# The last 512 tokens of a routed feed-forward run through all eight experts ahead of the item loop

## The chip, the cores and the metric

The kernel runs on one core of one Trainium2 chip. The metric is the device time of one execution in microseconds (us). Engines: PE is TensorE, DVE VectorE, ACT ScalarE, POOL GpSimd, SP the engine that issues most DMAs.

## What is computed

```python
h = _layernorm(x, axis=-1) * (1 + ca) + sa             # x: (2, 2048, 128)
x = x + ga * attention_block(h, Wq, Wm, W1, W2, g1, b1, g2, b2)   # linear attention and an MLP
h = _layernorm(x, axis=-1) * (1 + cb) + sb
x = x + gb * ffn(h, Wg, W1, W2)

def ffn(x, Wg, W1, W2):                                # Wg (128, 8), W1 (8, 128, 256), W2 (8, 256, 128)
    probs = softmax(xt @ Wg)                           # 4096 tokens, 8 experts
    _, top_idx = top_k(probs.T, 512)                   # each expert picks its 512 best tokens
    masked = where(sel, probs.T, -inf)
    tok2exp = where(sel.any(0), argmax(masked, 0), argmax(probs.T, 0))
    weights = probs[token, tok2exp]
    for e in range(8):
        gate = where(tok2exp == e, weights, 0)
        out += gate[:, None] * (gelu(xt @ W1[e], exact) @ W2[e])
```

So every token goes through exactly one expert, weighted by its probability. How many tokens an expert gets is known only on the chip. ga, gb and the other modulations come from a small matmul.

## The kernel before

All numbers are fp32. The 4096 tokens lie as 32 tiles of 128 (NT = 32), in 8 groups of 4 tiles (G, GT). The kernel has five engine programs, written out by hand in the order in which each engine executes; semaphores tie them.

**Attention and router (up to 137 us).** Each engine walks over the groups, software-pipelined. Results: x_sb (the stream after attention), h2 (the input of the experts), the router's logits in a bank of PSUM, and at the end h2T, the last two groups of h2 transposed. SP writes x_sb and h2 of each group to a table in DRAM (`table`, 256 numbers a token), POOL computes h2 for it (L348, L349) while the search runs.

**Search (from 140 us).** For each expert the 512th largest probability is found bit by bit, three bits a round, in ten rounds: DVE counts keys under four candidates (L1044), ACT under three (L517, Sign with a sum), PE adds the counts over partitions (L730, L733), DVE picks the digit (L1054, L1058). After round 0 ACT also casts the low halves of the keys (L522).

**Selection.** DVE finds which tokens each expert keeps, each token's expert, its rank within the expert by a scan along the tile, and with PE's sums over partitions (L735 to L754; `rbase_ready`) its slot in a list sorted by expert. Then the list is inverted with one-hot matrices: DVE builds them in four quarters of 8 tiles (L1120 to L1123), PE multiplies (L759), and DVE reads which token stands in each slot (L1136 to L1138: `gidx`). Before that read, DVE computes `eid`, the expert of each item (L1127 to L1133). A second pass of the same kind (`ohit`, `ohw`, L1149 to L1151, PE L794) gives the weight of every slot and item (L1156 to L1158).

**Item loop.** The sorted list is cut into 32 tiles. A tile that holds the end of an expert's tokens is run once for each expert in it, so there are at most NI = 32 + 7 = 39 items, and always 39 are run. Item i uses expert e = eid[i] and tile i - e. Per tile POOL gathers 128 rows of the table (L369, 16 of them ahead: R = 16), PE transposes them (p_xt, L766), ACT copies the result out of PSUM (L530). Per item SP loads the expert's W1 (L221, up to RW = 4 ahead), PE does the up matmuls (p_up, L773), ACT the GELU (L534), PE the down matmuls with W2 held in SBUF (p_down, L782), and DVE adds the weighted result to the tile's sum (add_item, L1166). From item LAG = 7 on, DVE also finishes tile i - 7 (finish, L1171 to L1178), and POOL scatters it to the output (L373) and then issues the gather of 16 tiles later:

```python
            for t in range(NT):
                gp.wait_ge(S["o_done"], t + 1)
                scatter(t)
                if t + R < NT:
                    gather(t + R)
```

PE's order in the loop is p_up(i + 1), p_xt(i + 2), p_down(i), and a down matmul waits until DVE has added item i - 2 (`y_free`):

```python
            for i in range(NI):
                e_next = p_up(i + 1) if i + 1 < NI else None
                if i + 2 < NT:
                    p_xt(i + 2)
                p_down(i, e_now)
                e_now = e_next
```

## Time and profile before

| | us |
|---|---|
| median of 3 runs (310.49 to 312.85) | 312.84 |
| the profiled execution | 311.66 |
| its span | 309.9 |
| PE busy in the span | 177.5 (57%) |
| DVE busy | 200.9 (65%) |
| ACT busy | 98.5 (32%) |
| POOL busy | 161.0 (52%) |

The span runs from the first to the last instruction of the profile; the execution's own time is 1.8 us longer. Times in rows are counted from the span's start. "Idle before" is the time in which the engine did nothing before this instruction, with the instruction that released it; "issue" means that the profile shows nothing that it waited for, "remote" an unknown source. In the table by stage, each engine's busy time stands with the number of its instructions, and PEclk is the granted share of PE's 2.4 GHz. An fp32 matmul stands as two records, so "x4" in rows of PE is two matmuls.

### The profile page before, as it was taken

What the parts mean: (1) busy time and instruction counts of PE and PEld (TensorE: products, weight loads), DVE (VectorE), ACT (ScalarE), POOL (GpSimd) and SP (SyncE); (2) the same over time, 40 slices, a digit from 0 to 9 for tenths busy, and PEclk for the clock granted to TensorE, in tenths of its full rate; (3) what the DMA queues carried; (4) which work ended last, traced back from release to release, by engine and by line L of the source; (5) the groups of instructions that cost most, each with busy time, mean ns of one, the idle gap of its engine ahead of it and who ended that gap; (6) DMA issues with size and microseconds to landing.
All of it is one profiled execution on the core that took longest, in us unless ns stands there. A gap on an engine that the chain in (4) does not pass through costs nothing.

```text
span 309.9 us, 4483 instructions
## 1 busy us (share of the span) xinstructions
PE 177.5 (57%) x1035; PEld 145.2 (47%) x1035; DVE 200.9 (65%) x701; ACT 98.5 (32%) x338; POOL 161.0 (52%) x229
## 2 busy tenths in 40 slices
PE   0878896596798895351112033527754574588730
PEld 0546684575586585351001022426644464577520
DVE  3789839949999988658897997013533253346660
ACT  1189843144265463115564002002221121222200
POOL 8645278917555334406991006770076665735552
PEclk9999997778699799555555555755995765758995
DMA  6940000000100000002662003432243333324210
GB/s 156 257 132 2 1 0 0 2 0 1 36 0 1 2 1 0 2 0 68 188 186 69 0 0 120 121 118 69 79 118 96 101 107 97 119 78 121 93 36 17
DMA packets 21721, 20.08 MB, mean 65 GB/s; under 512 B 2624, under 2 KB 19008, under 8 KB 21696
## 3 DMA queue, kind: packets, MB, share of 16 engines
q1 hardware_dynamic: 18144, 13.24, 14.7%
q0 software_dynamic: 2560, 6.30, 6.7%
q10 hardware_dynamic: 992, 0.27, 0.9%
q8 instruction: 9, 0.15, 0.2%
q14 instruction: 16, 0.13, 0.1%
HBM read 13.51 MB, written 6.29 MB: 64 GB/s over the span
## 4 chain that ended last, share of the span: by engine, by line
DVE 33%; PE 29%; another core or an unknown queue 13%; POOL 8%; issue 7%; ACT 6%; DMA 1%; DVEq 1%; POOLq 1%; ACTq 0%
PE pH L773 9%; DVE x_sb L965 6%; DVE hT L1044 5%; PE pQ L782 4%; POOL yr L244 3%; PE pH L675 3%; DVE bn L817 2%; ACT u L534 2%; PE pQ L668 2%; PE pQ L685 2%; POOL rs L244 2%; DVE xn L825 2%; PE pQ L567 2%; ACT x_sb L530 1%
## 5 line engine op out<-in xcount | busy, mean ns | idle before, releaser
L773 PE MATMUL pH<-x_sb,hid 128*128 (+1 forms) x156 | 35.9, 366 | 36.1 <-ACT x_sb L530 26.3
L373 POOL DMA_INDIRECT out_dram<-u,gidx x32 | 32.1, 1005 | 41.8 <-DVE u L1178 31.5
L369 POOL DMA_INDIRECT xn<-table_dram,gidx x32 | 33.6, 1051 | 33.2 <-DVE gidx L1138 23.8
L1166 DVE SCALAR_TENSOR_TENSOR h<-pQ,wslot,h 128x128 f32 (+1 forms) x39 | 13.7, 351 | 57.4 <-PE pQ L782 21.5
L773 PEld LDWEIGHTS pH<-x_sb,hid 128*128 128x128 f32 x156 | 27.1, 246 | 43.4 <-issue 43.4
L534 ACT ACTIVATE u<-pH 128x256 f32<-128x256 f32 x39 | 15.0, 384 | 80.7 <-remote 36.4
L782 PE MATMUL pQ<-ew,u 128*128 (+1 forms) x156 | 31.4, 337 | 3.9 <-issue 2.6
L782 PEld LDWEIGHTS pQ<-ew,u 128*128 128x128 f32 x156 | 27.6, 249 | 5.0 <-issue 4.7
L965 DVE SCALAR_TENSOR_TENSOR x_sb<-u,yr,x_sb 128x128 f32<-128x128 f32 x64 | 24.6, 445 | 4.4 <-POOL yr L244 4.1
L479 ACT ACTIVATE sqj<-pQ 128x128 bf16<-128x128 f32 x64 | 16.9, 278 | 28.4 <-POOL yr L244 12.3
L243 POOL TENSOR_SCALAR ve<-mv 128x4 f32<-128x4 f32 x16 | 3.3, 205 | 36.5 <-DVE mv L820 36.3
L825 DVE TENSOR_SCALAR xn<-x_sb,mv,rs 128x128 f32<-128x128 f32 x64 | 17.4, 336 | 3.5 <-POOL rs L244 3.5
L675 PE MATMUL pH<-qT,mall 128*128 128x512 f32 x32 | 19.0, 724 | 0.0
L685 PEld LDWEIGHTS pQ<-w,hid 128*128 128x128 f32 x128 | 16.0, 197 | 6.0 <-issue 6.0
L817 DVE BATCH_NORM_STATS2 bn<-x_sb 128x6 f32<-128x128 f32 x64 | 13.9, 280 | 6.1 <-DMA x_sb<-in_L_attn_x_dram 5.8
L685 PE MATMUL pQ<-w,hid 128*128 128x128 f32 x128 | 16.0, 280 | 1.9 <-DVE u L955 1.9
L668 PE MATMUL pQ<-mall,qT 128*128 128x128 f32 x64 | 12.2, 352 | 8.6 <-DVE u L950 8.6
L244 POOL TENSOR_TENSOR rs<-ve,neghalf 128x4 f32<-128x4 f32 x16 | 16.2, 1015 | 1.3
L348 POOL TENSOR_TENSOR t<-xn,cbR 128x512 f32<-128x512 f32 x8 | 10.1, 1266 | 11.2 <-DVE khi L1034 10.2
L668 PEld LDWEIGHTS pQ<-mall,qT 128*128 128x128 f32 x64 | 10.9, 255 | 9.9 <-issue 6.1
L244 POOL TENSOR_TENSOR yr<-yv,neghalf 128x8 f32<-128x8 f32 x8 | 13.1, 1639 | 0.7
L479 ACT ACTIVATION_READ_ACCUMULATOR sqj<-pQ 128x1 f32 x64 | 13.2, 207 | 0.0
(275 smaller groups left out, 441.2 us busy)
## 6 DMA issues: line engine op xcount, KB each, us to landing
hid<-in_L_ffn_W_dram SPq DMA_DIRECT2D x39, 128.0 KB
x_sb<-in_L_attn_x_dram SPq DMA_DIRECT2D x8, 256.0 KB, 6.5
table_dram<-x_sb SPq DMA_DIRECT2D x8, 256.0 KB, 2.8
table_dram<-h SPq DMA_DIRECT2D x8, 256.0 KB, 2.3
ew<-in_L_ffn_W_dram SPq DMA_DIRECT2D x2, 512.0 KB, 7.6
xn<-table_dram,gidx POOLq DMA_INDIRECT x32
out_dram<-u,gidx POOLq DMA_INDIRECT x32
wmod_sb<-in_L_wmod_dram SPq DMA_DIRECT2D x1, 384.0 KB, 4.9
```

What stands on the lines that cost most here:

```text
L244: return gp.tensor_tensor(dst, tmp, neghalf[:, 0:width], ALU.pow)
L369: gp.indirect_dma_start(row[:, t % R, :], None, table[:, :], bass.IndirectOffsetOnAxis(gidx[:, t:t + 1], 0), bounds_check=B * L - 1, oob_i ...
L373: gp.indirect_dma_start(out.rearrange("b l d -> (b l) d"), bass.IndirectOffsetOnAxis(gidx[:, t:t + 1], 0), o_sb[:, t % RO, :], None, bound ...
L479: last = act.activation(sqj[:, g % 2, k * GT + t, :], pQ[k][:, t * D:(t + 1) * D], ACT.Square, accum_out=ssq[:, g % 2, k * GT + t:k * GT + ...
L534: act.activation(eh[:, i % 2, :], pH[i % 2][:, 0:F], ACT.Gelu).then_inc(S["eh_done"], 1)
L668: mm = te.matmul(pQ0[:, t * D:(t + 1) * D], qT[:, g % 2, t * P:(t + 1) * P], mall[:, b, 0:D], start=True, stop=True)
L675: mm = te.matmul(pH[f][:, :], mall[:, b, D + f * P:D + (f + 1) * P], qT[:, g % 2, :], start=True, stop=True)
L685: mm = te.matmul(pQ1[:, t * D:(t + 1) * D], hid[:, g % 2, f, t * P:(t + 1) * P], w2[:, f, :], start=(f == 0), stop=(f == 1))
L773: mm = te.matmul(pH[i % 2][:, f * P:(f + 1) * P], wcur[:, i % RW, f * P:(f + 1) * P], xt[:, bass.ds(i - e, 1), :], start=True, stop=True)
L782: mm = te.matmul(pQ[i % 2][:, 0:D], eh[:, i % 2, f * P:(f + 1) * P], ew[:, bass.ds(e, 1), f * D:(f + 1) * D], start=(f == 0), stop=(f == 1))
L825: last = dve.tensor_scalar(xn[:, g, t, :], x_sb[:, g * GT + t, :], mv[:, g, t, 0:1], rs[:, g, t:t + 1], ALU.subtract, ALU.mult)
L965: last = dve.scalar_tensor_tensor(x1, u[:, t, :], yr[:, g % 2, n + t:n + t + 1], x1, ALU.mult, ALU.add)
```

## The change

The last group (tokens of tiles 28 to 31, DG = 7) leaves the sorted list and goes through all eight experts.

- **PE**: 16 up matmuls of 128x512 (`d_up`, weights w1d, input h2T of the last group) and 8 down steps of eight 128x128 matmuls (`d_down`). One such step stands after each round of the search, and the others between the matmuls of the selection and after the slot matmuls.
- **ACT**: 16 GELUs (`d_gelu`) and 8 copies out of PSUM (`d_copy`) in the same places. The activation table of GELU is loaded ahead of the search, no longer at the first item.
- **DVE**: during items 1 to 11 the eight results are summed with their weights (`dense_step`), multiplied by gb and added to x_sb.
- **SP**: loads all of W1 once (1 MB, at the start); stores the finished group in the loop, after the weight load of item 14.
- The list has 28 tiles (NP) and NI = 35 items, so 28 gathers and scatters. The quarters have 8, 8, 6 and 6 tiles.
- DVE reads the slots before it computes `eid`, and the weight pass is done in two halves, the first ahead of the first item's matmuls.
- POOL leaves out h2 of the last group; SP writes x_sb in its place.

```diff
-NI = NT + E - 1
+NI = NT - GT + E - 1
-NB = NT // 2
-QUARTERS = 4
+NP = NT - GT
+NB = NP // 2
+QUARTERS = (4, 4, 3, 3)
+DG = G - 1
...
+        def up_bank(k):
+            return (pH0, pQ1, pF)[k % 3]
...
+                if i == NP // 2:
+                    sp.wait_ge(S["out_d"], 1)
+                    sp.dma_start(out.rearrange("b (p t) d -> b p t d", p=P)[B - 1, :, TB - GT:TB, :], bgroup(x_sb, DG))\
+                      .then_inc(S["stored_d"], 16)
...
+            def d_gelu(k):
+                e = k // 2
+                act.wait_ge(S["up_d"], k + 1)
+                if e >= 2:
+                    act.wait_ge(S["down_d"], e - 1)
+                act.activation(ehd[e % 2][:, k % 2, :], up_bank(k)[:, :], ACT.Gelu).then_inc(S["gelu_d"], 1)
+
+            def d_copy(e):
+                act.wait_ge(S["down_d"], e + 1)
+                act.copy(yde[e], pQ0[:, :].rearrange("p (t d) -> p t d", d=D)).then_inc(S["copy_d"], 1)
+
+            d_gelu(0)
+            between = ((d_gelu, 1), (d_gelu, 2), (d_gelu, 3), (d_copy, 0), (d_gelu, 4), (d_gelu, 5), (d_copy, 1), (d_gelu, 6),
+                       (d_gelu, 7), (d_copy, 2))
...
+            def d_up(k):
+                e, f = k // 2, k % 2
+                if k >= 3:
+                    te.wait_ge(S["gelu_d"], k - 2)
+                te.matmul(up_bank(k)[:, :], w1d[:, e, f * P:(f + 1) * P], h2T[:, DG % 2, :], start=True, stop=True,
+                          skip_group_check=True).then_inc(S["up_d"], 1)
+
+            def d_down(e):
+                te.wait_ge(S["gelu_d"], 2 * e + 2)
+                if e:
+                    te.wait_ge(S["copy_d"], e)
+                for t in range(GT):
+                    for f in range(2):
+                        mm = te.matmul(pQ0[:, t * D:(t + 1) * D], ehd[e % 2][:, f, t * P:(t + 1) * P], ew[:, e, f * D:(f + 1) * D],
+                                       start=(f == 0), stop=(f == 1), skip_group_check=True)
+                mm.then_inc(S["down_d"], 1)
...
+            between = ((d_up, 2), (d_up, 3), (d_down, 0), (d_up, 4), (d_up, 5), (d_down, 1), (d_up, 6), (d_up, 7), (d_down, 2),
+                       (d_up, 8))
...
+            te.wait_ge(S["copy_d"], E)
...
+            p_weights(0)
             e_now = p_up(0)
...
+            link(dve.tensor_copy(inv[:, 0:2, 0:NP], pG[:, 0:2 * NP].rearrange("p (v j) -> p v j", v=2)))
+            link(dve.tensor_tensor(idf[:, 0:NP], inv[:, 0, 0:NP], inv[:, 1, 0:NP], ALU.add))
+            dve.tensor_copy(gidx[:, 0:NP], idf[:, 0:NP]).then_inc(S["slots_done"], 1)
+
             dve.wait_ge(S["rbase_ready"], 2)
...
+                    e = k - 1
+                    for t in range(GT):
+                        if e == 0:
+                            last = dve.tensor_scalar(accd[:, t, :], yde[e][:, t, :], wd[:, t, e:e + 1], None, ALU.mult)
+                        else:
+                            last = dve.scalar_tensor_tensor(accd[:, t, :], yde[e][:, t, :], wd[:, t, e:e + 1], accd[:, t, :], ALU.mult, ALU.add)
+                    last.then_inc(S["acc_d"], 1)
...
-                if i < 6:
+                if i < 5:
                     dve.memset(yacc[:, 8 + 4 * i:12 + 4 * i, :], 0.0)
+                if 1 <= i <= E + 3:
+                    dense_step(i - 1)
```

PE, rounds 1 to 3 of the search, before. L730 opens the sum in bank pG, L733 adds the counts.

```order
L730 MATMUL pG<-fill,onesb 128x7 [waits digits]
L733 MATMUL pG<-cnt,same16b 128x7 [waits counts,acounts]
L730 MATMUL pG<-fill,onesb 128x7 [waits digits]
L733 MATMUL pG<-cnt,same16b 128x7 [waits counts,acounts]
L730 MATMUL pG<-fill,onesb 128x7 [waits digits]
L733 MATMUL pG<-cnt,same16b 128x7 [waits counts,acounts]
```

The same three rounds now. L778 is an up matmul, L787 a down step.

```order
L804 MATMUL pG<-fill,onesb 128x7 [waits digits]
L807 MATMUL pG<-cnt,same16b 128x7 [waits counts,acounts]
L778 MATMUL pH<-h2T,w1d 128x512 [waits gelu_d]
L804 MATMUL pG<-fill,onesb 128x7 [waits digits]
L807 MATMUL pG<-cnt,same16b 128x7 [waits counts,acounts]
L787 MATMUL pQ<-ew,ex 128x128 [waits gelu_d]
L787 MATMUL pQ<-ew,ex 128x128 x7
L804 MATMUL pG<-fill,onesb 128x7 [waits digits]
L807 MATMUL pG<-cnt,same16b 128x7 [waits counts,acounts]
L778 MATMUL pQ<-h2T,w1d 128x512 [waits gelu_d]
```

Each round has gained an operation between the sum of its counts and the opening of the next. PE in the selection, from the last sums for the threshold (L742, L744) to the first slot matmuls (L759), before:

```order
L742 MATMUL pL<-scan,before 128x16 [waits rsum_ready]
L744 MATMUL pL<-scan,onesb 128x8
L748 MATMUL pF<-shift,onesb 128x16
L750 MATMUL pF<-rank,bmo 128x16 [waits rank_ready]
L752 MATMUL pF<-csum,onesb 128x16
L754 MATMUL pQ<-csum,onesb 128x8
L759 MATMUL pG<-feat,featT 128x64 [waits hi_ready] x32
```

And now (L830 is the matmul on the ranks, L843 the slot matmuls):

```order
L821 MATMUL pL<-scan,onesb 128x8
L787 MATMUL pQ<-ew,qT 128x128 [waits copy_d,gelu_d]
L787 MATMUL pQ<-ew,qT 128x128 x7
L778 MATMUL pQ<-h2T,w1d 128x512 [waits gelu_d]
L778 MATMUL pF<-h2T,w1d 128x512 [waits gelu_d]
L787 MATMUL pQ<-ew,ex 128x128 [waits copy_d,gelu_d]
L787 MATMUL pQ<-ew,ex 128x128 x7
L828 MATMUL pT<-shift,onesb 128x16
L830 MATMUL pT<-rank,bmo 128x16 [waits rank_ready]
L832 MATMUL pT<-csum,onesb 128x16
L834 MATMUL pH<-csum,onesb 128x8
L778 MATMUL pH<-h2T,w1d 128x512 [waits gelu_d]
```

Two down steps and two ups stand ahead of the matmul on the ranks, and one up (with a down step behind it) ahead of the slot matmuls. DVE, one early item of the loop (L1163 reads the item's expert), before:

```order
L1163 TENSOR_LOAD eid [waits y_free]
L1163 ISA x2
L1166 ISA [waits y_ready]
L1166 SCALAR_TENSOR_TENSOR h<-pQ,wslot,h 128x128
L1187 MEMSET h 128x512
```

And now:

```order
L1264 TENSOR_LOAD eid [waits y_free]
L1264 ISA x2
L1267 ISA [waits y_ready]
L1267 SCALAR_TENSOR_TENSOR h<-pQ,wslot,h 128x128
L1312 MEMSET h 128x512
L1288 SCALAR_TENSOR_TENSOR u<-feat,wd,u 128x128 [waits acc_d]
L1288 SCALAR_TENSOR_TENSOR u<-feat,wd,u 128x128 x3
```

Four operations on 128x128 follow the add and its memset.

## Rows read from the trace of the kernel before

**Rows 1.** Table by stage: us from and to, length, busy time of each engine, PEclk, DMA

```profile
137.00:187.00 50.00, 7.92 (x65) 5.16 (x65) 43.77 (x188) 17.30 (x64) 20.23 (x16) 0.50 0.27 79
187.00:211.00 24.00, 8.71 (x56) 7.62 (x56) 6.46 (x17) 3.18 (x8) 17.05 (x16) 0.57 0.41 121
228.00:275.00 47.00, 26.08 (x125) 23.39 (x124) 16.71 (x56) 7.90 (x28) 29.89 (x30) 0.66 0.35 105
```

**Rows 2.** Timeline of the search (start, us, engine, line, operation, idle before)

```profile
141.72 0.51 ACT L517 ACTIVATE hT<-khi,cur 128x256 bf16<-128x256 f32 x1 [3.10 <-DVE khi L1034]
...
148.60 0.17 PE L733 MATMUL pG<-cnt,same16b 128*128 128x7 bf16 x1 [1.63 <-DVE hT L1044]
149.29 0.19 PE L730 MATMUL pG<-fill,onesb 128*128 128x7 bf16 x1 [0.53 <-DVE cur L1058]
149.33 0.51 ACT L517 ACTIVATE hT<-khi,cur 128x256 bf16<-128x256 f32 x1 [0.92 <-DVE cur L1058]
...
151.11 0.17 PE L733 MATMUL pG<-cnt,same16b 128*128 128x7 bf16 x1 [1.62 <-DVE hT L1044]
```

**Rows 3.** Timeline of POOL in the loop, and one of the sums of ACT's waits

```profile
208.01 1.00 POOL L369 DMA_INDIRECT xn<-table_dram,gidx  x1 [0.30 <-issue]
224.36 1.02 POOL L373 DMA_INDIRECT out_dram<-u,gidx  x1 [15.35 <-DVE u L1178]
...
271.38 1.03 POOL L369 DMA_INDIRECT xn<-table_dram,gidx  x1 [0.30 <-issue]
...
ACT u L534 <- remote: 36.4, 7, 8.8
```

**Rows 4.** DVE: timeline of the loop; a group of the lines; a piece of the chain

```profile
213.99 0.35 DVE L1166 SCALAR_TENSOR_TENSOR h<-pQ,wslot,h 128x128 f32 x1 [1.95 <-PE pQ L782]
...
222.23 0.35 DVE L1166 SCALAR_TENSOR_TENSOR h<-pQ,wslot,h 128x128 f32 x1 [1.29 <-PE pQ L782]
...
273.77 0.35 DVE L1166 SCALAR_TENSOR_TENSOR h<-pQ,wslot,h 128x128 f32 x1 [5.66 <-PE pQ L782]
...
301.37 0.35 DVE L1166 SCALAR_TENSOR_TENSOR h<-pQ,wslot,h 128x128 f32<-128x128 f32 x1 [0.34 <-issue]
...
L1187 DVE MEMSET h<- 128x512 f32 x6 | 2.9, 485 | 0.3
...
126.56 1.15 DVE x_sb L965 x4
```

**Rows 5.** Chain (59 to 65 us), timeline of PE (88 to 91 us), one group of ACT

```profile
59.54 2.05 PE pQ L668 x8
61.59 3.41 PE pH L675 x4
...
88.17 1.88 PE L675 MATMUL pH<-qT,mall 128*128 128x512 f32 x4
89.89 1.95 PE L685 MATMUL pQ<-w,hid 128*128 128x128 f32 x16
...
L472 ACT ACTIVATE hid<-pH 128x512 f32<-128x512 f32 x8 | 4.8, 605 | 5.7 <-PE pH L675 5.6
```

**Rows 6.** Timeline from the last quarter to the first item

```profile
183.98 0.61 PE L759 MATMUL pG<-feat,featT 128*128 128x64 bf16 x8 [0.73 <-DVE featT L1123]
...
185.81 0.22 DVE L1136 COPY inv<-pG 128x64 f32<-128x64 f32 x1
...
187.39 1.30 POOL L369 DMA_INDIRECT xn<-table_dram,gidx  x1 [23.77 <-DVE gidx L1138]
...
190.70 0.45 PE L766 MATMUL pT<-ident,xn 128*128 128x128 f32 x1 [6.12 <-DMA xn<-table_dram,gidx]
...
191.53 1.28 ACT L534 ACT_TABLE_LOAD   x1
```

**Rows 7.** Timeline of PE around the ranks and the first two quarters

```profile
176.11 0.20 PE L750 MATMUL pF<-rank,bmo 128*128 128x16 bf16 x1 [5.22 <-DVE csum L1096]
...
179.98 0.61 PE L759 MATMUL pG<-feat,featT 128*128 128x64 bf16 x8 [3.63 <-DVE featT L1123]
181.31 0.61 PE L759 MATMUL pG<-feat,featT 128*128 128x64 bf16 x8 [0.73 <-DVE featT L1123]
```

More of the change, by code:

```diff
@@ L261, in _ @@
             gp.memset(segmask[:, :], 1.0)
+            gp.memset(oh[:, :, B - 1, TB - GT:TB], 0.0)
             gp.memset(same16b[:, :], 1.0)
@@ L360, in _ @@
             gp.wait_ge(S["keys"], 1)
-            for g in range(G):
+            for g in range(DG):
                 h2tok(g)
@@ L522, in _ @@
                     act.copy(klo[:, :], ki[:, 1, :]).then_inc(S["klo_ready"], 1)
+                step, what = between[n]
+                step(what)
             act.wait_ge(S["over_ready"], 1)
@@ L1150, in _ @@
-            for v in range(3):
-                last = dve.tensor_tensor(ohw[:, :, v, :, :], ohit[:, :, :, :], pair(val[:, 2 + v, :], NI), ALU.mult)
-            last.then_inc(S["ohw_ready"], 1)
+            half = NB // 2
+            for h in range(2):
+                bs, ts = slice(h * half, (h + 1) * half), slice(2 * h * half, 2 * (h + 1) * half)
+                link(dve.tensor_tensor(ohit[:, bs, :, :], count_to(NI, half), pair(item[:, ts], NI), ALU.is_equal))
+                for v in range(3):
+                    last = dve.tensor_tensor(ohw[:, bs, v, :, :], ohit[:, bs, :, :], pair(val[:, 2 + v, ts], NI), ALU.mult)
+                last.then_inc(S["ohw_ready"], 1)
```

173 lines of the change are left out of this document (118 added, 55 removed).

## The prediction, made before the changed kernel was run

> **What bounds the kernel now.** I read the table by stage first. From 137 to 187 us (search and selection) TensorE (PE) is busy 7.92 of 50.00 us, at a granted clock of 0.50, which is 1.2 of 2.4 GHz, and DVE 43.77 us: DVE's chain sets this stage [rows 1]. Next, the timeline of one search round: the matmul that sums the counts (L733) starts at 148.60 and again at 151.11, so a round is 2.51 us; PE idles 1.62 us right before it, and ACT 0.92 us before the first of its three count operations [rows 2]. Those gaps are where the new work goes. From 187 us on, the item loop. PE is busy only 8.71 of 24.00 us up to 211 and 26.08 of 47.00 us from 228 to 275 [rows 1]; ACT waits 36.4 us in 7 pieces for something that the profile doesn't name [rows 3]. These stretches coincide with the gathers: item 2 is added only at 213.99, right after the first 16 gathers, and from the first scatter at 224.36 to the last gather at 271.38 the loop again goes slowly [rows 3, 4]. DVE's adds at 222.23 (item 7) and 273.77 (item 23) lie 51.54 us apart, 3.22 us an item. After that, with no gather left, items 23 to 38 take 27.60 us, 1.84 us each, which is DVE's own pace [rows 4]. So a slot that needs no gather inside the loop is worth 3.22 us, but one after the gathers only 1.84.
>
> **The change, part by part.** The change adds one end of the work (512 tokens through eight experts) and takes four items off the other.
>
> *Prices of one dense step.* An up matmul is 128x512 fp32. Two cost 3.41 us at the low clock and 1.88 at the high one, so 1.71 or 0.9 us each. A down step is eight 128x128 matmuls: 1.95 us for eight at the high clock; at the low one four took 2.05 us, so 4.1. One GELU or copy over 512 columns on ACT is like L472: 0.6 us [rows 5].
>
> *Search.* In rounds with an up matmul PE needs 1.71 us at most, and between one L733 and the next there are 2.51 less 0.17 and 0.19, so 2.15 us: hidden at either clock. A down step stands in three rounds. At 1.95 us it is hidden; at 4.1 us each makes its round 1.9 us late. That is 0 to 5.7 us; I take 2.0, as the clock should be high for part of it. On ACT a 0.6 us operation fits into the gap of 0.92 us, except in round 0, where ACT also casts the low keys: 0.6 us late. First GELU and table load: ACT idles 3.10 us before the first count operation, and the load of 1.28 us plus 0.6 fit; it was beside the first item before, where it delayed little: 0 [rows 2, 6]. Search: +2.6 us.
>
> *Selection.* Before its matmul on the ranks (L750, 176.11) PE idles 5.22 us [rows 7]. Two downs and two ups now stand there: 5.7 us at the high clock, 11.6 at the low one. So L750, for which DVE waits with everything behind it, is 0.5 to 6.4 us late; I take 1.5, plus 0.2 for the up matmuls beside the threshold. Behind L750 one up and one down come before the first slot matmul, which is 3.87 us later (179.98) [rows 7]: 2.9 us fit, 5.8 do not. Two more ups stand between the quarters, whose pitch is 1.33 us. I take 0.5 late at the end. Two gains: the quarters shrink from 32 tiles and 64 columns to 28 and 56, about 0.8 of 5.3 us; and DVE reads the slots (L1136, 185.81) as soon as PE has them. Now the last quarter's matmul ends at 184.59 (183.98 + 0.61) and DVE first computes the piece numbers; 1.2 us go [rows 6]. Gathers start at +2.6 + 1.7 + 0.5 - 0.8 - 1.2 = **+2.8 us**.
>
> *Start of the loop.* After the slot matmuls PE still owes one up, two downs and the waits for ACT's two copies, 0.9 + 3.9 + 1.2 = 6.0 us, and only then comes the first transpose (now at 190.70). The slot matmuls would end at 184.59 + 2.8 + 1.2 = 188.6, so the transpose at 194.6: 3.9 us late, against a first gather that lands 3.3 us after its start [rows 6], at 193.5. But items 0 to 2 are held until the 16 gathers are through, and these are 2.8 late. So +2.8 stands for item 2 as well. The halved weight pass has its matmuls in the same slow stretch: 0.
>
> *Dense sums on DVE.* Eight steps of four operations, 1.15 us a step as in L965 [rows 4], about 1.25 with its wait, in items 2 to 9, and smaller ones in items 1, 10 and 11. From item 2 to item 7 the loop has 8.24 us, 1.65 an item, PE's pace, in which DVE has an idle gap ahead of each add: 1.29 us in item 7, where no memset stands, of which some 0.6 are the reading of the piece number. Where a memset of 0.485 us also stands, little is free [rows 4]. Three items at about +1.0 and two at +0.55: **+4.1 us**. For items 7 to 11 DVE has added 1.25 us each while PE is being held anyway, and DVE has up to two finished items in hand: I take +1.0 of 0 to 5.
>
> *SP.* After the weight load of item 14 SP waits for the dense sum (item 11 on DVE), then stores 256 KB, and the loads of items 15 and later are queued behind. PE is at most two items ahead of DVE, so a load that now comes four items early comes just in time: 0 to 3 us, I take 0.5. POOL loses one pair of operations in the search: 0, it is not waited for.
>
> *Four items less.* They go out of the stretch at 3.22: the gathers within the loop fall from 16 to 12, and the 16 items behind the last gather remain. 4 x 3.22 = **-12.9 us**; at the tail's pace it would be 4 x 1.84 = -7.4.
>
> *Sum.* 2.8 + 4.1 + 1.0 + 0.5 - 12.9 = -4.5 us, against the profiled execution of 311.66 us (span 309.9): 307.2, call it **307 us**. The median of the runs shown is 312.84, so that is 1.9% below it.
>
> **The clock, and one rule of the skill that speaks against the change.** The row of 137 to 187 us shows 0.50 with PE almost idle; from 228 to 275, with PE busy just over half, it is 0.66 [rows 1]. The Trainium skill, TensorE: Matmul & The Clock Gate, Part 1, says the default state is throttled and activity releases it. By it the dense work would lift its own clock, but must first run slow; if it never lifts, the sum is that of the first rival. The Trainium skill, ScalarE: Activation LUTs, What ACT_TABLE_LOAD costs, gives about 2.66 us a switch with its drain, the trace 1.28 for the load; by the page the first count operation would be some 0.2 us late. ACT's order has one such load before and after, so GELU between the counts brings no more.
>
> **The rivals.**
> *The clock stays low (slower).* PE's dense work then overruns every gap: 0.6 + 5.7 in the search, 6.4 + 0.9 around the ranks, 2.0 at the quarters, less 2.0 gained: +13.6 us for the gathers, in place of 2.8. Total 311.66 + 13.6 + 5.6 - 12.9 = 318.0. For it: 50 us at 0.50. Against: with 16 ups and 8 downs PE has 60 us of low-clock work, so it would hardly idle. It decides once the start is later than +12.
>
> *The saved items are worth the tail's pace (no change).* If the slow stretch is set by something else than the count of gathers, four items give 7.4: 311.66 + 8.4 - 7.4 = 312.7. For it: the engines are held by a cause that I can't name. Against: nothing slows the loop once the gathers are over.
>
> *All is hidden (faster still).* At the high clock the gathers start 0.6 - 2.0 = -1.4 us, stage costs 4.1 + 1.0: 311.66 - 1.4 + 5.1 - 12.9 = 302.5. Against: one down at the low clock is enough to lose 1.9 us.
>
> **How the numbers follow.** Forecast 0.45, clock low 0.15, tail's pace 0.20, all hidden 0.20. Beyond about 1% (3.1 us) a difference can be told from none. The forecast spreads by the search (0 to 5.7), the ranks (0.5 to 6.4), SP (0 to 3) and DVE (0 to 5), and is faster by over 1% in some 85 of 100. Faster 0.38 + 0.20 + 0.02 = 0.60; same 0.06 + 0.16 = 0.22; slower 0.15 + 0.03 = 0.18. The range reaches from below the third rival, 300, to 316, which leaves out most of the first.
>
> **What would show it.** Rounds of 2.5 us in the search except those with a down step (up to 4.4); a granted clock above 0.50 from about 145 us; the idle time of DVE before its read of the rank sums; gathers starting near 190; items 3 to 9 at 2.2 to 3.1 us on DVE; 12 gathers within the loop and 16 items of 1.84 us behind them. I am wrong if the gathers start before 188 or after 195, if DVE's dense steps cost the loop under 2 or over 8 us, or if the stretch with gathers takes as long with 12 of them as with 16.

## The result, and the profile after

The changed kernel takes **299.50 us** (median of 4 runs, 299.04 to 300.37), the kernel before in the same session 312.85 us (310.49 to 314.11). The ratio is 0.9591, 95% interval 0.9549 to 0.9633: 4.1% less. The prediction was 307.0 us, range 300 to 316. So the sign was right, the gain between the profiled executions (12.1 us) was nearly three times the forecast 4.5, and the time lies just under the range.

| | before | after |
|---|---|---|
| profiled execution, us | 311.66 | 299.52 |
| span, us | 309.9 | 297.8 |
| mean granted clock of TensorE | 0.749 | 0.828 |
| first gather issued, us | 187.39 | 186.19 |
| item 2 added | 213.99 | 214.21 |
| item 7 added | 222.23 | 222.45 |
| last gather issued | 271.38 | 260.47 |
| last item added | 301.37 | 289.87 |

The table by stage of the kernel after (us from and to, length, busy time and instructions of PE, PEld, DVE, ACT and POOL, granted clock, DMA share, GB/s), against [rows 1]:

```profile
137.00:187.00 50.00, 38.43 (x205) 24.46 (x204) 42.45 (x191) 30.34 (x87) 18.53 (x15) 0.83 0.28 80
187.00:211.00 24.00, 8.80 (x68) 7.52 (x67) 5.76 (x19) 2.74 (x8) 15.77 (x16) 0.67 0.41 121
228.00:265.00 37.00, 20.08 (x96) 17.02 (x96) 16.08 (x53) 5.83 (x21) 24.05 (x23) 0.70 0.36 111
```

In search and selection TensorE is busy 38.43 us in place of 7.92, at a mean granted clock of 0.83 in place of 0.50, and DVE's own 42.45 us still fill the stage.

The timelines of PE and ACT in the search, kernel after (start, us, engine, line, operation, idle before), against [rows 2, 5, 6]:

```profile
138.62 1.28 ACT L538 ACT_TABLE_LOAD   x1
...
141.70 0.51 ACT L554 ACTIVATE hT<-khi,cur 128x256 bf16<-128x256 f32 x1 [1.19 <-DVE khi L1127]
```

```profile
148.86 0.17 PE L807 MATMUL pG<-cnt,same16b 128*128 128x7 bf16 x1 [0.42 <-DVE hT L1137]
148.88 3.03 PE L787 MATMUL pQ<-ew,ex 128*128 128x128 f32 x16
...
157.64 3.60 PE L787 MATMUL pQ<-ew,qT 128*128 128x128 f32 x16
...
166.27 2.02 PE L787 MATMUL pQ<-ew,ex 128*128 128x128 f32 x16
...
176.89 0.19 PE L830 MATMUL pT<-rank,bmo 128*128 128x16 bf16 x1
```

L787 is a down step. Two of the three in the search ran partly at the low clock (3.03 and 3.60 us) and the third at the high one (2.02 us). The granted clock over these stretches (table by stage, columns as above):

```profile
146.00:149.00 3.00, 2.25 (x6) 0.86 (x6) 2.30 (x13) 2.67 (x10) 2.78 (x3) 0.50 0.69 200
149.00:152.00 3.00, 3.00 (x20) 2.99 (x20) 2.24 (x13) 1.78 (x8) 2.78 (x3) 0.67 0.71 199
155.00:158.00 3.00, 0.92 (x6) 0.56 (x5) 2.72 (x14) 2.06 (x7) 2.78 (x3) 0.97 0.70 200
158.00:160.00 2.00, 2.00 (x12) 2.00 (x11) 1.96 (x10) 1.59 (x6) 1.78 (x3) 0.50 0.54 153
162.00:187.00 25.00, 20.16 (x143) 13.97 (x141) 22.43 (x94) 12.95 (x34) 0.81 (x1) 1.00 0.11 31
```

It came up during the first down step, fell back by the second, after PE had been busy for only 0.92 us from 155 to 158, and was full from 162 on. The table load and the first GELU ended before ACT's first count operation, which starts at 141.70 as before at 141.72. The rank matmul is 0.78 us later than before (176.89 against 176.11, [rows 7]).

From the last quarter to the first gather, kernel after (timelines of DVE and POOL), against [rows 6]:

```profile
184.62 0.21 DVE L1229 COPY inv<-pG 128x56 f32<-128x56 f32 x1
```

```profile
186.19 1.50 POOL L392 DMA_INDIRECT xn<-table_dram,gidx  x1 [25.32 <-DVE gidx L1231]
...
206.34 1.00 POOL L392 DMA_INDIRECT xn<-table_dram,gidx  x1 [0.30 <-issue]
225.63 1.01 POOL L396 DMA_INDIRECT out_dram<-u,gidx  x1 [18.29 <-DVE u L1303]
226.95 1.04 POOL L392 DMA_INDIRECT xn<-table_dram,gidx  x1 [0.30 <-issue]
...
251.16 1.01 POOL L396 DMA_INDIRECT out_dram<-u,gidx  x1 [3.67 <-DVE u L1303]
...
260.47 1.03 POOL L392 DMA_INDIRECT xn<-table_dram,gidx  x1 [0.30 <-issue]
```

The gathers start 1.2 us earlier than before, not 2.8 later. In the loop, the stretch from the first scatter to the last gather is 260.47 - 225.63 = 34.84 us for 12 gathers; before it was 271.38 - 224.36 = 47.02 us for 16 [rows 3]. That is 2.90 and 2.94 us a pair of scatter and gather. From the last gather to the last add it is 29.40 us, before 29.99. The whole difference of 11.5 us at the last add is then: first scatter 1.27 later, this stretch 12.18 shorter, the rest 0.59 shorter. Of the 12.18 us some 10.3 are eight steps fewer of POOL, and 1.9 are pauses of POOL (5.7 us of them before, 3.8 after). From the issue of the last scatter to the end of the span it is 5.86 us, before 6.51, which is another 0.65 us.

DVE's adds, kernel after, against [rows 4] (items 2, 7, 12 and 34):

```profile
214.21 0.35 DVE L1267 SCALAR_TENSOR_TENSOR h<-pQ,wslot,h 128x128 f32 x1 [0.94 <-PE pQ L872]
...
222.45 0.35 DVE L1267 SCALAR_TENSOR_TENSOR h<-pQ,wslot,h 128x128 f32 x1
...
236.22 0.35 DVE L1267 SCALAR_TENSOR_TENSOR h<-pQ,wslot,h 128x128 f32 x1 [0.70 <-issue]
...
289.87 0.35 DVE L1267 SCALAR_TENSOR_TENSOR h<-pQ,wslot,h 128x128 f32<-128x128 f32 x1 [0.34 <-issue]
```

Item 2 to item 7 takes 8.24 us, exactly as before, though five items now carry steps of the dense sum.

### The profile page after: what moved, and what is told of

Its sections match the earlier page's. It is cut to its first block, busy times and chain, and to the rows that moved or that the text cites. A ratio compares the mean times of both kernels' runs of the same rounds, so it can differ in the third digit from the quotient of the medians.

```text
span 297.8 us, 4671 instructions
## 1 busy us (share of the span) xinstructions
PE 200.4 (67%) x1151; PEld 156.1 (52%) x1151; DVE 202.8 (68%) x725; ACT 108.9 (37%) x354; POOL 150.0 (50%) x220
## 4 chain that ended last, share of the span: by engine, by line
PE 34%; DVE 30%; issue 17%; POOL 8%; ACT 5%; another core or an unknown queue 2%; DVEq 1%; POOLq 1%
PE pH L863 7%; DVE x_sb L1058 6%; PE pQ L787 5%; DVE hT L1137 4%; POOL yr L266 3%; PE pQ L872 3%; PE pH L726 3%; DVE bn L910 3%; PE pQ L719 2%; PE pQ L736 2%; POOL rs L266 2%; DVE xn L918 2%; ACT u L585 2%; PE pQ L618 2%
## 5 line engine op out<-in xcount | busy, mean ns | idle before, releaser
L863 PE MATMUL pH<-x_sb,hid 128*128 (+1 forms) x140 | 30.8, 354 | 31.5 <-issue 21.5
L396 POOL DMA_INDIRECT out_dram<-u,gidx x28 | 28.5, 1017 | 41.0 <-DVE u L1303 30.4
L392 POOL DMA_INDIRECT xn<-table_dram,gidx x28 | 29.0, 1035 | 33.5 <-DVE gidx L1231 25.3
L863 PEld LDWEIGHTS pH<-x_sb,hid 128*128 128x128 f32 x140 | 23.1, 235 | 38.3 <-issue 38.3
L585 ACT ACTIVATE u<-pH 128x256 f32<-128x256 f32 x35 | 13.4, 383 | 74.7 <-PE pH L863 31.0
L1267 DVE SCALAR_TENSOR_TENSOR h<-pQ,wslot,h 128x128 f32 (+1 forms) x35 | 12.3, 350 | 38.2 <-PE pQ L872 13.7
L872 PE MATMUL pQ<-ew,u 128*128 (+1 forms) x140 | 26.9, 324 | 7.0 <-issue 4.4
L872 PEld LDWEIGHTS pQ<-ew,u 128*128 128x128 f32 x140 | 23.1, 234 | 9.1 <-issue 8.8
L502 ACT ACTIVATE sqj<-pQ 128x128 bf16<-128x128 f32 x64 | 16.8, 277 | 28.4 <-POOL yr L266 12.2
L265 POOL TENSOR_SCALAR ve<-mv 128x4 f32<-128x4 f32 x16 | 3.3, 204 | 36.5 <-DVE mv L913 36.4
L719 PE MATMUL pQ<-mall,qT 128*128 128x128 f32 x64 | 12.1, 351 | 8.6 <-DVE u L1043 8.6
L371 POOL TENSOR_TENSOR t<-xn,cbR 128x512 f32<-128x512 f32 x7 | 8.9, 1267 | 11.0 <-DVE khi L1127 10.2
## 6 DMA issues: line engine op xcount, KB each, us to landing
w1d<-in_L_ffn_W_dram SPq DMA_DIRECT2D x1, 1024.0 KB, 10.3
```

Source lines behind the costliest of these rows:

```text
L392: gp.indirect_dma_start(row[:, t % R, :], None, table[:, :], bass.IndirectOffsetOnAxis(gidx[:, t:t + 1], 0), bounds_check=B * L - 1, oob_i ...
L396: gp.indirect_dma_start(out.rearrange("b l d -> (b l) d"), bass.IndirectOffsetOnAxis(gidx[:, t:t + 1], 0), o_sb[:, t % RO, :], None, bound ...
L502: last = act.activation(sqj[:, g % 2, k * GT + t, :], pQ[k][:, t * D:(t + 1) * D], ACT.Square, accum_out=ssq[:, g % 2, k * GT + t:k * GT + ...
L719: mm = te.matmul(pQ0[:, t * D:(t + 1) * D], qT[:, g % 2, t * P:(t + 1) * P], mall[:, b, 0:D], start=True, stop=True)
L863: mm = te.matmul(pH[i % 2][:, f * P:(f + 1) * P], wcur[:, i % RW, f * P:(f + 1) * P], xt[:, bass.ds(i - e, 1), :], start=True, stop=True)
L872: mm = te.matmul(pQ[i % 2][:, 0:D], eh[:, i % 2, f * P:(f + 1) * P], ew[:, bass.ds(e, 1), f * D:(f + 1) * D], start=(f == 0), stop=(f == 1))
```

## The experiments

They ran on two chips (one for runs 1 to 4, one for runs 5 to 12), and the first thing they showed is that the ground had changed: the kernel before takes 283.9 us on the one and 284.6 us on the other, in place of 312.85. Which chip the first measurement ran on is not on record; the texts call it the first chip. The ratio of the change is the same. The kernels before and after were therefore profiled again, as runs 5 and 6. In the expectations, a "chip like the first" is one at 312.85 us.

The ratio behind each time is to the kernel before of the same session, with its 95% interval. The changed kernel itself was not run again on the chip of runs 1 to 4, so for these runs "under the changed kernel" sets their time against run 6 on the other chip, and a difference under about 1.5 us is not clear of noise (the intervals reach 0.4 to 0.6% to either side). One profiled execution also differs from the next ahead of the loop: the same code issued its first gather between 185.74 and 187.18 us in nine of them (kernel after, and runs 1 to 3, 6 to 8, 11 and 12).

**Runs 5 and 6: the kernels before and after again.** No edit.

> The kernel before, unchanged, for its profile on the chip of these experiments. On the chip of the first experiments it took 283.9 us instead of 312.85. If what went is the late signals of TensorE during the gathers, the first item is added 6.5 us after the first gather was issued plus the gather's own latency, near 196 us (213.99 in the first profile, item 2), items 0 to 7 go at 1.7 us each, and POOL issues a scatter and a gather each 2.65 us without a pause between the first scatter and the last gather, which ends items 16 on. On a chip like the first one it is 311 to 313 us with item 2 at 214.

> The changed kernel, unchanged. Ratio to before 0.95 to 0.96 whichever chip it is: about 271.5 us where before takes 284, 299.5 where it takes 312.85. Theory P (in the loop POOL's chain of indirect transfers, 1.31 us each, is what the four tiles cost: 8 transfers, 10.5 us) and theory I (the items cost what the items cost, 1.82 us each, 7.3 us for four) both have to reach the difference of 12 us: under P POOL's pause between issues is nil up to the last gather and items 16 on wait for gathers.

Measured: before 284.61 us (ratio 0.9994, 0.9969 to 1.0019), after **272.15 us** (0.9562, 0.9522 to 0.9602). The same first 190 us as on the first chip, and then a loop without its stalls. ACT's timeline, first the kernel after on the first chip, then the same kernel here (L585 is the GELU of an item, which waits for the up matmuls):

```profile
196.58 0.38 ACT L585 ACTIVATE u<-pH 128x256 f32<-128x256 f32 x1 [5.23 <-remote]
...
208.62 0.38 ACT L585 ACTIVATE u<-pH 128x256 f32<-128x256 f32 x1 [11.50 <-remote]
```

```profile
192.53 0.38 ACT L585 ACTIVATE u<-pH 128x256 f32<-128x256 f32 x1 [1.22 <-PE pH L863]
...
194.18 0.38 ACT L585 ACTIVATE u<-pH 128x256 f32<-128x256 f32 x1 [1.11 <-PE pH L863]
```

So the waits of 36.4 us for something unnamed [rows 3] are not a property of the kernel. POOL's transfers in the loop, kernel before, then kernel after, on this chip (timelines):

```profile
208.13 1.00 POOL L369 DMA_INDIRECT xn<-table_dram,gidx  x1 [0.30 <-issue]
212.14 1.02 POOL L373 DMA_INDIRECT out_dram<-u,gidx  x1 [3.01 <-DVE u L1178]
213.46 1.04 POOL L369 DMA_INDIRECT xn<-table_dram,gidx  x1 [0.30 <-DVE u L1178]
...
253.43 1.03 POOL L369 DMA_INDIRECT xn<-table_dram,gidx  x1 [0.30 <-issue]
...
276.63 0.98 POOL L373 DMA_INDIRECT out_dram<-u,gidx  x1 [0.59 <-issue]
```

```profile
209.91 1.01 POOL L396 DMA_INDIRECT out_dram<-u,gidx  x1 [2.18 <-DVE u L1303]
...
241.49 1.03 POOL L392 DMA_INDIRECT xn<-table_dram,gidx  x1 [0.30 <-issue]
...
264.71 0.98 POOL L396 DMA_INDIRECT out_dram<-u,gidx  x1 [0.59 <-issue]
```

Each transfer holds POOL about 1.0 us, and the next starts 0.30 us behind it: a scatter and a gather take 2.65 us. Before, POOL runs so without a pause from 212.14 to past 253.43 (the 15 pairs between its first and last gather in the loop take 39.97 us, 2.66 each), while the items could go at 1.82 us. From there to the end both kernels need the same: the last add stands 21.15 us behind the issue of the last gather before, and 21.16 after. The first add came at 198.34 us in run 5, 2.3 us later than expected. DVE's adds show the price of the dense sums, which have no stalls to hide behind here: item 7 to item 12 takes 9.16 us before (210.01 to 219.17) and 13.74 us after (206.73 to 220.47).

**Run 1: no late weight loads.** 

```
             for i in range(NI):
-                e = sp.value_load(...)
-                if i >= RW:
-                    sp.wait_ge(S["up_ready"], i - RW + 1)
-                sp.dma_start(wcur[:, i % RW:i % RW + 1, :], ...)
                 if i == NP // 2:
                     ...                                    # the store of the finished group, as before
+                if i >= RW:
+                    continue
+                e = sp.value_load(...)
+                sp.dma_start(wcur[:, i % RW:i % RW + 1, :], ...)
```

> The changed kernel, with the loop's weight loads on SP left out after the first four items, so later items use the first weights still in the buffers (left out: the right W1 of items 4 to 34; all transfers of 128 KB on SP's queue after the fourth go). Theory G (the gathers of POOL alone set the pace of items 7 to 19): within 1% of 299.5 us, items 7 to 20 still take some 42 us. Theory W (gathers and weight loads share the transfer engines, and it is their sum that holds): 10 to 20 us less, items 7 to 20 at 2.0 to 2.5 us each.

Measured: 272.43 us (0.957, 0.9516 to 0.9624) against 272.15 for the changed kernel: no difference. The weight loads don't set the time, but one of them is late in the loop. SP waits for the dense sum before it stores the finished group, and the next weight load stands behind that store (issued at 218.89 and 219.99 us in run 6). PE waits for it:

```profile
223.00 1.22 PE L863 MATMUL pH<-x_sb,hid 128*128 x4 [3.27 <-DMA hid<-in_L_ffn_W_dram]
```

Items 12 to 14 take 5.07 us in run 6 and 3.64 here, where that load is left out. The 1.4 us are lost again by the end, as the gathers are as late (runs 2 and 3). The expected 42 us for items 7 to 20 were those of the first chip (41.88); here they are 28.4 us.

**Run 2: no gathers in the loop.** 

```
             for t in range(NP):
                 gp.wait_ge(S["o_done"], t + 1)
                 scatter(t)
-                if t + R < NP:
-                    gather(t + R)
```

> The changed kernel without the 12 gathers that POOL issues inside the loop; the tiles 16 to 27 take the rows of tiles 0 to 11 (left out: the fetch of those rows). If the gathers in the loop hold items 7 to 19 (my prediction's 3.22 us for each item against 1.82 without them), these 13 items go at 1.82 to 1.9 us and the time is 284 us, 15 less. If the loop is held by the chain PE, ACT, DVE of an item, less than 3 us comes off. Items 0 to 2, behind the first 16 gathers, stay where they are in either case.

PE's wait for a gather is adapted to it. Measured: 270.72 us (0.9514, 0.9465 to 0.9562), only 1.4 us under the changed kernel. From item 16 on the items go at 1.82 us, yet nearly the same end is reached. So after the change the gathers in the loop are hardly a bound any more: something else is as late. Run 3 shows what.

**Run 3: no dense sums on DVE.** 

```
-                if 1 <= i <= E + 3:
-                    dense_step(i - 1)
```

SP's wait for the dense sum ahead of the store goes with them.

> The changed kernel without the eleven steps on DVE that weigh and sum the experts' outputs of the last 512 tokens (left out: those sums; the store of these tokens stays, and no longer waits). The dense work on PE and ACT stays. My prediction's term for these steps was 4.1 us in items 2 to 7: by it item 7 ends 4 us earlier and the time is 295 to 296 us. By the reading of the trace after (item 2 to item 7 took 8.24 us with and without them) item 7 moves by under 0.5 us and the time stays within 0.5% of 299.5 us.

Measured: 271.05 us (0.9533, 0.9475 to 0.9592), 1.1 us less, not clear of noise. Inside it moves more than that. Item 7 is where it was (207.65 us, 206.73 in run 6, whose loop began 0.9 us earlier), so the steps at items 1 to 6 are free, as the trace after had said. But item 7 to item 12 takes 9.16 us in place of 13.74: the five steps at items 7 to 11, where the output operations stand as well, cost 0.92 us each. Items 12 to 14 take 3.64 us in place of 5.07, as the late weight load of run 1 is gone too. Most of these 6.0 us is given back later: item 20 to item 24 alone takes 10.69 us in place of 7.42, each add waiting for a row whose gather POOL has only just issued. The timeline of PE in run 3:

```profile
236.56 0.71 PE L862 MATMUL pH<-x_sb,hid 128*128 x4 [0.45 <-issue]
238.40 0.48 PE L855 MATMUL pF<-ident,xn 128*128 128x128 f32 x1 [1.14 <-DMA xn<-table_dram,gidx]
```

**Run 4: no dense work.** All calls of `d_up`, `d_gelu`, `d_down`, `d_copy` and `dense_step` left out.

> The changed kernel with no dense work at all (left out: the experts of the last 512 tokens, on PE, ACT and DVE; the loop has 35 items as before the edit). My prediction charged that work 2.6 us in the search, 1.9 us of lateness in ranks and quarters, 2.8 us at item 2 and 4.1 us for the sums: by it the first gather starts some 4 us earlier and the time is about 291 us. By the reading of the trace after, where the clock was already up for most of it, the search ends 0.9 us earlier, the first gather starts 0.5 to 1.0 us earlier (185.3 us), unless the engine's clock falls without that work, and the time is 298 to 299 us.

Measured: 269.42 us (0.9462, 0.9412 to 0.9511), 2.7 us under the changed kernel, more than the 0.5 to 1.5 us expected. The first gather starts at 185.49 against 186.13. The search and selection stage:

```profile
137.00:187.00 50.00, 7.50 (x61) 4.81 (x61) 43.71 (x194) 17.28 (x64) 19.19 (x15) 0.50 0.27 79
```

PE's 31 us of dense work cost the gathers 0.64 us between these two executions, and by the spread of the nine others 0.3 to 1.7. Of the 9.9 us that my prediction's terms put on the dense work (2.6 + 1.7 + 0.5 + 4.1 + 1.0), 2.7 reach the end, through POOL: its last gather is issued at 238.89 in place of 241.49.

**Run 7: eight more gathers.** The kernel after, with POOL's count of indirect transfers back at 64, and nothing else.

```
                 if t + R < NP:
                     gather(t + R)
+                if t < 8:
+                    gp.indirect_dma_start(spare[t], None, table[:, :],
+                                          bass.IndirectOffsetOnAxis(gidx[:, t:t + 1], 0), ...)
```

> The changed kernel with eight more indirect gathers on POOL, one behind each of the first eight scatters, into buffers that nobody reads: POOL issues again 64 indirect transfers, as before the change; items, tiles and all other work stay at 35. Theory P (POOL's chain sets the end): 8 x 1.31 = 10.5 us slower, 282 us or 310 us, as slow as before within 1%. Theory I (the four items themselves): the same as the changed kernel within 1%.

Measured: **283.31 us**, 11.2 us slower than the changed kernel, and within 0.5% of the kernel before (0.9954, 0.9932 to 0.9977). Theory P holds: give POOL its eight transfers back and the gain is gone, although four items, their weights, their matmuls and their outputs stay away. What is left of the gain, 1.3 us, is about the earlier start of the gathers. POOL in this run:

```profile
209.84 1.02 POOL L398 DMA_INDIRECT out_dram<-u,gidx  x1 [2.18 <-DVE u L1308]
211.16 1.05 POOL L394 DMA_INDIRECT xn<-table_dram,gidx  x1 [0.30 <-issue]
212.52 1.01 POOL L410 DMA_INDIRECT pe_<-table_dram,gidx  x1 [0.31 <-issue]
...
275.11 0.98 POOL L398 DMA_INDIRECT out_dram<-u,gidx  x1 [0.59 <-issue]
```

From first gather to last scatter it is 275.11 - 186.16 = 88.95 us, before (run 5) 276.63 - 187.56 = 89.07, after (run 6) 264.71 - 186.13 = 78.58. The difference of the last two is 10.49 us, which is 8 x 1.31. The rest of the 11.2 us stands behind the last scatter: from its issue to the end of the span it is 6.52 us here and in run 5, and 5.86 in run 6. That piece goes by the number of indirect transfers in every trace (4.88 us with 44 of them, 5.21 with 48, 5.86 with 56, 6.51 or 6.52 with 64), 0.08 us for each.

**Run 8: the dense sums early.** 

```
+DENSE = {0: (2,), 1: (3,), 2: (4,), 3: (5,), 4: (6,), 5: (7, 8), 6: (9, 10)}
...
-                if 1 <= i <= E + 3:
-                    dense_step(i - 1)
+                for k in DENSE.get(i, ()):
+                    dense_step(k)
```

Steps 0 and 1 stand ahead of the wait for the weights (`inv_ready`, 3).

> The changed kernel with the DVE steps of the dense sums moved ahead: steps 0 and 1 in DVE's wait ahead of the loop, the others at items 0 to 6, so that none stands beside the output steps of items 7 to 11. The result is the reference's. Items 7 to 12 then go at 1.83 us in place of 2.75 (4.6 us earlier at item 12). Theory P: gathers of POOL hold items 16 to 26 instead, and 1 to 2 us of it remain in the time. Theory D (DVE holds the loop): 4 us remain. On a chip like the first, item 7 is late by the signals of TensorE, and 0 to 4 us remain.

Measured: 271.90 us (0.9552, 0.9513 to 0.9591), the same as the changed kernel within its uncertainty. Item 7 is 1.7 us later (208.44), item 12 is 2.3 us earlier (218.17), and items 20 to 24 take 10.54 us where POOL has not yet issued their gathers. Less than the 1 to 2 us of theory P is left; theory D is out.

**Run 9: one part of the change alone.** The kernel before, with the slots (`inv`, `idf`, `gidx`) read ahead of `endi`, `enext`, `eid`, the first operations on the weights moved ahead of that read, and the weight pass in two halves.

> The kernel before with one part of the change alone: slots read ahead of the piece numbers and the weight pass in two halves (all four tiles of the last 512 tokens stay sparse; the result is the reference's). The first gather should start 1.2 us earlier (186.3 in place of 187.56). Theory P (POOL's chain of 64 indirect transfers runs from there almost without a pause to the last scatter): the time falls by the same 1.0 to 1.3 us, 283.4 where before takes 284.6. If the start is not on the path (items wait elsewhere in between): no change, within 0.2%.

Measured: 282.63 us (0.9926, 0.9903 to 0.9949), 2.1 us less, more than the 1.2 expected. The first gathers of run 5 and of run 9:

```profile
187.56 1.30 POOL L369 DMA_INDIRECT xn<-table_dram,gidx  x1 [23.74 <-DVE gidx L1138]
```

```profile
185.72 1.56 POOL L369 DMA_INDIRECT xn<-table_dram,gidx  x1 [22.57 <-DVE gidx L1136]
```

1.84 us earlier, of which 1.17 are the order (POOL's wait is 23.74 and 22.57 us); in the rest (0.65 us) the two executions differ already before the edit, at the first slot matmul. Of the 1.84 us, 1.57 are left at the last scatter (275.06 against 276.63): the start is on the path. The medians' 2.1 us (1.4 to 2.8 by the interval) is more than the 1.17 of the order, and why is open. The halved weight pass seems to help too: item 0 is added 2.82 us earlier (195.52 against 198.34), more than the gathers' 1.84, and POOL's pause ahead of its first scatter falls from 3.01 to 2.44 us.

**Run 10: the kernel before without gathers in the loop.** The edit of run 2, on the kernel before.

> The kernel before without the 16 gathers inside the loop; later tiles take rows of earlier ones (left out: the fetch of these rows). Theory P: items 16 to 38 go at 1.82 us in place of 2.16 on the mean (226.96 to 274.58), the last item is added near 267, 8 us earlier, and the time is 276 to 277 us; items alone bound it then, and the four that the change saves would be worth 7.3 us. If the items' own chain holds it: under 2 us.

Measured: 275.45 us (0.9666, 0.9633 to 0.9699), 9.2 us under before; the last item is added at 266.84 in place of 274.58. Beside run 2 this makes a square: with the gathers in the loop the change gives 284.61 - 272.15 = 12.5 us, without them 275.45 - 270.72 = 4.7 us (runs 10 and 2, on two chips whose kernel before differs by 0.8 us). The latter is what the items alone give, by the adds of runs 10 and 2: item 7 is added 2.84 us earlier, the items behind item 14 take 7.50 us less, being four fewer, the sums at items 7 to 11 take 4.65 more and the late weight load 0.95: together 4.74.

The square also bounds theory P. With 39 items and not one gather in the loop the kernel takes 275.45 us, 3.3 us more than the changed kernel with its 56 transfers. So by run 10 a change that only took eight transfers away could give 9.2 us at most; the rest of the 12.5 comes from items that start earlier and are four fewer.

**Run 11: gathers ahead of scatters.**

```
-            for t in range(NP):
-                gp.wait_ge(S["o_done"], t + 1)
-                scatter(t)
-                if t + R < NP:
-                    gather(t + R)
+            for t in range(NP - R):
+                gp.wait_ge(S["o_done"], t + 1)
+                gather(t + R)
+                if t % 2:
+                    scatter(t // 2)
+            for t in range((NP - R) // 2, NP):
+                gp.wait_ge(S["o_done"], t + 1)
+                scatter(t)
```

> The changed kernel, with POOL issuing each loop gather ahead of the scatters (two gathers, then one scatter, until the last gather; then the other scatters); the result is the reference's. The last gather should be issued near 233 in place of 241.5 us. POOL's chain stays 56 x 1.31 us long, so it ends 0 to 3 us earlier, as its pauses are closed. Since without any loop gather the time fell by 1.4 us only, items and DVE hold it as well: 270.5 to 271.5 us where the changed kernel takes 272.15.

Measured: 274.55 us (0.964, 0.9605 to 0.9674), **2.4 us slower** than the changed kernel; my expectation was wrong. The scatters held back left POOL with nothing to do while items came at 2.88 us (the dense sums) and while PE waited for the late weight load of run 1 (4.30 us here, 3.27 in run 6), and they are owed at the end:

```profile
210.10 0.99 POOL L392 DMA_INDIRECT xn<-table_dram,gidx  x1 [1.94 <-DVE u L1306]
212.98 1.00 POOL L392 DMA_INDIRECT xn<-table_dram,gidx  x1 [1.88 <-DVE u L1306]
...
265.67 0.98 POOL L396 DMA_INDIRECT out_dram<-u,gidx  x1 [0.30 <-issue]
266.96 0.98 POOL L396 DMA_INDIRECT out_dram<-u,gidx  x1 [0.30 <-issue]
```

The last scatter follows the one before it by 1.29 us: POOL is still catching up when the last item is done (263.90). It comes 3.06 us behind the last add, in run 6 2.06. So of 2.25 us at the last scatter 1.0 are owed scatters, and 1.25 stand already at the last add; they arise at items 12 to 16, behind the late weight load. That the order of the transfers lengthened this wait fits but is not shown. From 228.74 us on POOL issues without a longer pause than 0.50 us, so a pause before that is not made good, as theory P says.

**Run 12: both edits.** Run 8 and run 11 together.

> Both edits together: gathers ahead of scatters and the dense sums on DVE at items 0 to 6; the result is the reference's. Theory P with a second bound beside it (each edit alone gains little because the other bound is as late): together items 12 to 34 go at 1.82 us, the last item is added at 218.2 + 22 x 1.82 = 258.2, POOL's chain then ends some 3 us earlier than now, near 262, and the time is 268.5 to 269.5 us, 2.5 to 3.5 less. If only the sum of single gains holds: 270.5 to 271.

Measured: **269.69 us** (0.9487, 0.9454 to 0.952), 2.5 us under the changed kernel, though run 8 alone gained nothing and run 11 alone lost. The last item is added at 257.66, 5.0 us earlier, and the last scatter is issued at 261.69, 3.0 us earlier. That is 0.2 us above the expected range, and every run of it is below every run of the single edits (269.28 to 270.75 against 271.64 and more). From first gather to last scatter it is 75.95 us; 55 steps of 1.31 are 72.1, and of the 4 us between them only 1.2 are pauses, the rest are transfers that held POOL longer. The last scatter comes 4.0 us behind the last add, in run 6 2.06, so POOL's chain ends this version, and fewer transfers could bring some 2 us before the items, at 1.82 us each from item 12 on, hold it. It is the best version found.

## Why the prediction was wrong

Two steps of the sum failed: the dense sums on DVE in items 2 to 7, priced at +4.1 us, cost nothing, and the delay of item 2, priced at +2.8 us, was 0.22. The parts in order:

- **Search, +2.6 us.** The later end of the search is 0.93 us (the threshold is ready at 169.33 against 168.40). The mechanism was right: the rounds with a down step that ran partly at the low clock (3.03 and 3.60 us) are 0.4 and 1.1 us longer, where I had charged 1.9 for each step at the low clock. The third step ran at the high clock and cost nothing. Of ACT's 0.6 us 0.23 came, in round 0. The table load made nothing late: GELU starts 1.29 us behind the load's start (139.91), and the first count operation is on time, so the 0.2 us named for a drain did not come. That makes 1.7 us, and 0.7 of them were given back by luck. One DVE operation halfway (L1064, now L1157) takes 1.30 us before and 0.61 after, and in both ends at 155.65, some 0.3 us behind the end of the POOL operation beside it (155.37 and 155.36):

```profile
154.35 1.30 DVE L1064 SCALAR_TENSOR_TENSOR klo<-khi,cur,klo 128x256 f32<-128x256 f32 x1
...
155.04 0.61 DVE L1157 SCALAR_TENSOR_TENSOR klo<-khi,cur,klo 128x256 f32<-128x256 f32 x1
```

  With this work the granted clock of the stage is 0.83. By the Trainium skill, TensorE: Matmul & The Clock Gate, Part 1, activity releases the throttle; the trace agrees (0.50 without this work, run 4, and 0.83 with it).
- **Ranks and quarters, +1.7 and +0.5.** Mis-sized: next to nothing. The four steps ahead of the ranks ran at the high clock, as in the lower end of my range. The rank matmul is 0.78 us later, which is less than the search was.
- **Slots first and smaller quarters, -1.2 and -0.8.** Right: between the first slot matmul (0.74 us late) and the last quarter's (0.14 late) the quarters gain 0.6, and run 9 gives 1.17 us for the order. The first gather is 1.2 us earlier in all. The sum for the gathers was +2.8 and should have been -1.2.
- **Start of the loop, +2.8 at item 2.** Measured +0.22. The 6.0 us from the end of the slot matmuls to the first transpose were right: measured 6.2 (184.45 to 190.69). But the slot matmuls ended at 184.45 and not at 188.6, so the transpose is at 190.69, before at 190.70, and the 3.9 us of lateness did not come. The rule that items 0 to 2 follow the 16 gathers did not hold to the microsecond: the 16th gather is 1.67 us earlier (206.34 against 208.01) and item 2 is 0.22 later. On the first chip that stays open. In runs 5 and 6 item 2 is 3.0 us earlier.
- **Dense sums, +4.1 in items 2 to 7.** Wrong step: measured 0 on the first chip (8.24 us both times) and 0 by run 3. DVE's idle gap ahead of an add, of which I counted 0.6 us as lost to the reading of the piece number, is free for other work: with a step's four operations queued ahead of the add, it falls to 0.19 us (item 7 in run 6, below). The price stands in items 7 to 11, where the output operations are, and it is 4.6 us where nothing hides it (runs 3 and 6). I had +1.0 of 0 to 5 there; on the first chip it is about nil, since before the change those items were held as long anyway (14.21 us before, 13.77 after).
- **SP, +0.5 of 0 to 3.** The mechanism was right, and it costs 1.4 us in the loop of run 6 (items 12 to 14, run 1). On the first chip PE waits 3.29 us for the same load, and items 12 to 14 take 5.08 us in place of 5.03: other waits stood there before.
- **Four items at 3.22, -12.9.** The size was nearly right, and the reason too narrow. On the first chip the stretch with gathers became 12.18 us shorter, of which some 10.3 are eight indirect transfers of POOL and 1.9 its pauses. Run 7 puts the transfers at 10.5 us and 0.65 behind the last scatter. The rival of the tail's pace (7.4 us) is refuted by run 7, and run 10 shows where it would hold: in a kernel with no gathers in the loop.
- **The sum.** On the first chip: item 2 +0.22, items 2 to 7 0.00, from there to the last add -11.72, behind the last scatter -0.65, in all -12.15 in the span. The forecast's -4.5 misses item 2 by 2.6 us, the sums by 4.1, the end behind the last scatter by 0.65, which had no term, and the rest by 0.3. That -1.2 for the earlier gathers and -10.5 for the transfers come to nearly the same total (-11.7) is a coincidence there, as the earlier gathers did not bring item 2 forward. In runs 5 and 6 it is no coincidence: the first gather is 1.43 us earlier, from first to last gather it is 10.51 less, from there to the last add the same, and 0.66 less behind the last scatter, in all 12.6 in the span.

I had named two signs of being wrong, gathers starting before 188 us and sums that cost under 2 us, and both came true. The clock rival (318.0) is out. The rival nearest to the outcome was "all is hidden" with 302.5, and it too had 5.1 us for the sums.

What stays open: theory P was tested on two chips without the unnamed stalls. On the first chip POOL had pauses of up to 3.67 us in the loop, so its chain was not closed there; that eight steps fewer make 10.3 of the 12.2 us fits, but run 7 was not made on it.

The change does what the Trainium skill asks for in DMA: Bandwidth & Descriptors, SWDGE vs HWDGE vs iDMA: plain transfers go to SP or ACT and only irregular ones to GpSimd. Four tiles of scatter became one plain store on SP, four tiles of gather went away with them, and run 7 shows what that is worth here: 1.31 us of POOL for each indirect transfer.

## What to carry to other kernels

Count the indirect transfers and multiply: an engine whose timeline says "0.30 idle, issue" before every instruction is full, even if its busy share reads 50%, and work taken off the others gives little until its chain gets shorter. Then ask what stands next: here the items were only 9.2 us behind. Before pricing added work from an idle gap, ask whether the gap is a wait or only the reading of a register, which other queued work covers. A store that waits for a result holds back every load queued behind it (3.27 us of PE in run 6). When two bounds end together, single edits show nothing or a loss (0.2 better, within noise, and 2.4 worse) and only both together gain.

## What the runs showed of the hardware that I had not expected

- **One kernel, 10% apart.** The kernel before: 312.85 us in the first session, 283.9 and 284.6 on the two chips of the runs. What sets them apart isn't shown. Up to the first gather they agree (187.39 and 187.56 us). The difference arises in the loop, while POOL issues gathers: item 0 of the kernel after is added at 209.39 us there and at 195.06 here. On the first chip ACT waits up to 11.50 us for a signal of matmuls that PE's own record shows as done; in that trace fewer semaphore events of the up matmuls are recorded (28, and 36 in run 6), and fewer of all kinds (2299, and 3236), so "remote" may stand for a releaser that wasn't recorded. The cause is open; the program and its transfers are the same on both.
- **The granted clock came up within the search, and fell once more.** The first down step at 148.88 took 3.03 us and the one at 157.64 took 3.60, but that at 166.27 took 2.02; the stage's mean is 0.83. In the loop before the change, with PE busy about half of the time, it stood at 0.66 [rows 1].
- **An indirect transfer is paid for twice.** Each holds POOL's chain for 1.31 us, and each adds 0.08 us between the issue of the last scatter and the end (4.88 us with 44 transfers, 6.52 with 64).
- **A DVE operation that ends with POOL's.** L1064 (L1157 after) ends 0.28 or 0.29 us behind the end of the POOL operation beside it, whether it takes 1.30 us or 0.61 (also in run 9, with 1.29, and run 12, with 0.75), so it seems to wait for POOL.
- **A DVE pause is not always idle time.** In run 6 the gap ahead of an add is 0.56 us where the output operations, which wait on one another, come before it, and 0.19 us where a dense step's operations do:

```profile
206.73 0.35 DVE L1267 SCALAR_TENSOR_TENSOR h<-pQ,wslot,h 128x128 f32 x1 [0.19 <-PE pQ L872]
...
209.61 0.35 DVE L1267 SCALAR_TENSOR_TENSOR h<-pQ,wslot,h 128x128 f32 x1 [0.56 <-issue]
```

In the first DVE waits for PE and the reading of the piece number is covered; the second I read as that reading with nothing to cover it.
